# Keys, queries and attention values of a node bucket computed in the gather stage, one bucket ahead, instead of in the sort's rounds

## The chip, the cores and the metric

The kernel runs on one core of a Trainium2 chip. The metric is the device time of one launch in microseconds (us). Five engines work side by side and meet at semaphores: TensorE (PE, its weight loads shown apart as PEld), VectorE (DVE), ScalarE (ACT), GpSimd (POOL) and SyncE (SP, which here only issues DMAs).

## The reference

One relational graph layer over 6250 nodes, 200,000 edges and 16 relations, width 128. `h` is the layer norm of `x` after a relu. Every edge has a value that depends on its source node and relation alone:

```python
semb = h[src] @ tokeys.T ; oemb = h[src] @ toqueries.T ; pemb = relations[rel]
values = exp(sum(semb * pemb * oemb, axis=1) / 128)
fr = src + n * rel
values = values / segment_sum(values, fr)[fr]
output = segment_sum(values[:, None] * h[dst], fr)          # (r, n, e)
weights = einsum('rb,bij->rij', comps, bases_w)
out = x + relu(einsum('rij,rnj->ni', weights, output))
```

So per node n and relation r there is one number V[n, r] = exp(sum over e of key[n, e] * query[n, e] * relation[r, e] / 128).

## The kernel before, in words

**Tiling.** The nodes are cut into NB = 49 buckets of 128. The edges are cut into NCH = 50 chunks. Two stages follow each other.

**The sort's rounds** (`run_steps`, 52 steps, on every engine a function `step`). Step i does two things side by side. It handles bucket i: ACT normalises its nodes (`normalise`, L979), PE turns them (`transpose_h`, L1174), ACT applies the relu (`relu_ht`, L986), PE makes keys and queries (`keys_queries`, L1191 and L1192) and the messages h @ W_r for all 16 relations (`messages`, L1199, eight matmuls of 512 columns), ACT copies them out (`copy_z`, L1034) and SP stores them to the table `Z` in HBM (L301). And it sorts chunk i into streams of records by source bucket: one-hots and prefix sums on DVE (L563 to L655) and PE (L1152, L1163 to L1167, L1184), the record scatter on POOL (L453). The keys and queries go from PSUM bank 6 to SBUF by ACT (`copy_so`, L1008), are multiplied by POOL (`key_query`, L461) and multiplied by the relations on PE inside `records` (L1210, into bank 3); ACT takes the exp into `V` (L1024). Each engine runs its own list strictly in order. PE's order in a step is: transpose, sums (L1152), compact (L1184), keys and queries, prefix (L1163 to L1167), messages, records (L1210 to L1212).

**The gather stage** (after `bad < 1`; one `stepb(b)` per bucket on PE and DVE, one `bucket(b)` on ACT and SP, one `gather(b)` on POOL). SP joins the two streams of a bucket and loads its records (L322, L327). PE turns them (`turn_records`, L1267), DVE decodes them (L738) and makes the gather indices (`gather_index`, L776). POOL issues 31 to 33 indirect DMAs per bucket (L492), each of which brings 128 message rows from `Z` into one tile of `Gbuf[b % 2]`; it may start bucket b only when the sum of bucket b - 2 has been taken (`acc`). PE counts (`tables`, L1276), turns one-hots (L1286, semaphore `tp`), sums the counts (`sum_counts`, L1297 and L1298, semaphore `cs`), adds up the gathered tiles of the bucket before (`aggregate(b - 1)`, L1319, 36 tiles as 72 matmul records into bank 2, semaphore `acc` at its end) and looks the weights up (`lookups`, L1307). DVE reads the counts (`own_counts`, L784 to L790), makes the weights from V and the counts (`weights`, L799 to L815, first wait: `cs`), the one-hots of the next bucket (`tables`, L745 to L768), the output rows of the bucket before (`finish`, L833, waits for `acc`) and the weighted one-hots (`weighted_onehot`, L825). ACT copies the turned one-hots to SBUF (L1101, waits for `tp`), spreads the next bucket's relations (L1080) and copies one shared tile (L1091).

**What sets the order around the change.** All orders are written out by hand; there is no planner. PE in `stepb(b)`: turn_records(b + 1), tables(b), sum_counts(b), aggregate(b - 1), lookups(b). DVE: records(b + 1), gather_index(b + 1), own_counts(b), weights(b), tables(b + 1), finish(b - 1), weighted_onehot(b). ACT: the three copies of L1101, spread_relations(b + 1), shared_tile(b).

Of the kernel before, what the change touches and what calls it, by code (L numbers as in the profile page):

```python
# [6 lines left out]
ACT = mybir.ActivationFunctionType  # L7
# [25 lines left out]
def program(nc, x, src, dst, rel, tokeys, toqueries, relations, comps, bases_w, out):  # L33
# [40 lines left out]
    with ExitStack() as ctx:  # L74
# [3 lines left out]
        def sem(name):  # L78
# [136 lines left out]
            h th ht so_mm so_sb prod z_mm z_sb zst0 zst1 zrow v ends ends_mm nt nt_total nt_mm nt_row shared act_go join sp_go marks_sb marks_st  # L215
# [167 lines left out]
        def _(pool):  # L383
# [72 lines left out]
            def key_query(i, par):  # L456

                pool.wait_ge(s["so_sb"], i + 1)
                if dyn(i) or i >= 2:
                    pool.wait_ge(s["rec_mm"], i - 1)  # L460
                g.tensor_tensor(PR[par][:], SO[:, 0:P], SO[:, P:2 * P], ALU.mult).then_inc(s["prod"], 1)  # L461

            def step(i, par):
                if dyn(i) or 1 <= i <= NB:
                    key_query(i - 1, 1 - par)
# [57 lines left out]
        def _(dve):  # L523
# [206 lines left out]
            bad = dve.value_load(ROWI[0:1, 3 * NB:3 * NB + 1], min_val=0, max_val=16 * NB)  # L730
            with dve.If(bad < 1):
# [46 lines left out]
                def own_counts(b):  # L778
# [90 lines left out]
                gather_index(0, 0)  # L869
                tables(0, 0)  # L870
# [8 lines left out]
            with dve.If(bad > 0):  # L879

# [68 lines left out]
        def _(act):  # L949
# [54 lines left out]
            def copy_so(i):  # L1004
                act.wait_ge(s["so_mm"], i + 1)
                if dyn(i) or i >= 1:
                    act.wait_ge(s["prod"], i)
                a.copy(SO[:], bank[6][:, 0:2 * P]).then_inc(s["so_sb"], 1)  # L1008

# [7 lines left out]
            def copy_rec(i, par):  # L1017
# [5 lines left out]
                if dyn(i) or i < NB:  # L1023
                    a.activation(V[:, bass.ds(i, 1), :].rearrange("p a r -> p (a r)"), bank[3][:, 256:256 + R],  # L1024
                                 ACT.Exp, scale=1.0 / EMB).then_inc(s["v"], 1)
                else:
                    a.copy(stats[0:1, 0, 0:1], stats[0:1, 0, 1:2]).then_inc(s["v"], 1)
# [11 lines left out]
            def step(i, par, zt):  # L1039
# [10 lines left out]
                if dyn(i) or i < NB:  # L1050
                    copy_so(i)
# [21 lines left out]
            bad = act.value_load(ROWI[0:1, 3 * NB:3 * NB + 1], min_val=0, max_val=16 * NB)  # L1073
            with act.If(bad < 1):
# [19 lines left out]
                def bucket(b, par):  # L1094
# [8 lines left out]
                    if dyn(b) or b + 1 < NB:  # L1103
                        spread_relations(b + 1, 1 - par)
                        shared_tile(b, par)

                spread_relations(0, 0)
# [7 lines left out]
            with act.If(bad > 0):  # L1115
                with act.Fori(0, NCOL) as t:
# [4 lines left out]
        def _(pe):  # L1121
# [48 lines left out]
            def transpose_h(i):  # L1170
                pe.wait_ge(s["h"], i + 1)
                if dyn(i) or i >= 1:
                    pe.wait_ge(s["so_sb"], i)
# [15 lines left out]
            def keys_queries(i, par):  # L1189
                pe.wait_ge(s["ht"], i + 1)  # L1190
                t_.matmul(bank[6][:, 0:P], KQT[:, 0, :], HT[par][:], start=True, stop=True)  # L1191
                t_.matmul(bank[6][:, P:2 * P], KQT[:, 1, :], HT[par][:], start=True, stop=True)\  # L1192
                    .then_inc(s["so_mm"], 1)

            def messages(i, par):
# [6 lines left out]
            def records(i, par):  # L1202

                pe.wait_ge(s["d_sb"], i + 1)
                if dyn(i) or i >= 1:
                    pe.wait_ge(s["rec_sb"], i)
                    pe.wait_ge(s["v"], i)
# [198 lines left out]
```

## Time and profile before

| | |
|---|---|
| Time, median of 3 runs | 3077.86 us (3076.86 to 3082.03) |
| The profiled execution's own time | 3066.26 us |
| Its span | 3064.5 us |
| Mean granted TensorE clock | 0.673 |
| PE / PEld busy | 51% / 37% |
| DVE / ACT / POOL busy | 44% / 15% / 54% |
| Sort's rounds | about 50 to 390 us |
| Gather stage | about 420 to 3062 us |

The span runs from the first to the last instruction; 1.8 us of the execution lie around it. A busy share is an average over both stages. On the page PE, DVE and the DMA traffic are high in the first five of 40 slices (the rounds) and then fall to a flat pattern (the gather stage). "Issue" and "remote" in a view of waits mean that the profile shows no releaser that came last. A matmul's end is modelled, its start is recorded.

### The profile page before, as it was taken

To read this page: it belongs to the slowest core of one execution; us is meant where nothing else is said; L and a number is where in the kernel's file an instruction comes from. 1 tells how busy PE (TensorE), PEld (TensorE's weight loads), DVE (VectorE), ACT (ScalarE), POOL (GpSimd) and SP (SyncE) were. 2 spreads that over 40 slices of the span, in tenths; PEclk is the share of its full clock that TensorE was granted. 3 is DMA by queue.
4 is the path that set the end of the run, shared out by engine and by line. 5 is a ranking of instruction groups with operands and counts; after the bars stand their busy time and mean duration, and the time that the engine had idled before them with its cause. 6 is when DMAs were issued, how large, how long until landed. Compare 5 with 4: busy or idle time off the path is not lost.

```text
span 3064.5 us, 32426 instructions
## 1 busy us (share of the span) xinstructions
PE 1549.4 (51%) x9121; PEld 1129.2 (37%) x9122; DVE 1354.7 (44%) x2385; ACT 462.7 (15%) x918; POOL 1651.2 (54%) x1804
## 2 busy tenths in 40 slices
PE   4999932444344454534454443544444444544435
PEld 3666621233233333323333332333333333333324
DVE  7999934334243433424343342434334243433423
ACT  4666611000010100001010000101000010101000
POOL 3444444655646465555646565564655556464653
PEclk8999965656666665666666566666656566666667
DMA  5444411111111111111111111111111111111111
GB/s 154 156 155 155 155 55 32 46 41 42 45 36 45 36 46 39 43 42 41 45 36 45 38 44 43 40 45 37 45 38 43 44 39 45 36 46 36 45 42 29
DMA packets 99825, 170.47 MB, mean 56 GB/s; under 512 B 32491, under 2 KB 48612, under 8 KB 99575
## 3 DMA queue, kind: packets, MB, share of 16 engines
q0 software_dynamic: 51776, 104.48, 13.1%
q1 hardware_dynamic: 47672, 65.57, 6.3%
q10 hardware_dynamic: 352, 0.14, 0.0%
q8 instruction: 10, 0.16, 0.0%
q14 instruction: 15, 0.12, 0.0%
HBM read 112.24 MB, written 59.59 MB: 56 GB/s over the span
## 4 chain that ended last, share of the span: by engine, by line
another core or an unknown queue 40%; issue 21%; DVE 20%; PE 14%; SPq 2%; DMA 2%; DVEq 1%; ACT 0%; POOLq 0%; ACTq 0%
PE bank L1199 6%; DVE arena L825 4%; DVE CX L790 3%; PE bank L1184 2%; DVE stage L768 2%; DVE WC L801 2%; DVE pay_all L784 1%; PE bank L1152 1%; PE bank L1276 1%; DVE OHR L766 1%; PE bank L1319 1%; DMA RL<-bucket_streams 1%; DVE pay_all L815 1%; PE bank L1307 1%
## 5 line engine op out<-in xcount | busy, mean ns | idle before, releaser
L492 POOL DMA_INDIRECT arena<-Z_messages,IDX x1568 | 1483.0, 946 | 1137.4 <-issue 955.1
L1319 PE MATMUL bank<-arena 128*128 128x128 f32 x3528 | 695.2, 353 | 733.1 <-issue 724.9
L1319 PEld LDWEIGHTS bank<-arena 128*128 128x128 f32 x3528 | 632.5, 264 | 797.3 <-issue 795.3
L799 DVE TENSOR_SCALAR WC<-bank 128x128 f32<-128x128 f32 x49 | 14.3, 292 | 1150.5 <-remote 1149.2
L1101 ACT COPY pay_all<-bank 128x1024 bf16<-128x1024 bf16 x147 | 108.0, 807 | 2136.6 <-remote 2059.9
L1307 PE MATMUL bank<-pay_all 128*128 128x256 bf16 x882 | 179.8, 347 | 310.9 <-DVE arena L825 249.1
L825 DVE TENSOR_TENSOR arena<-stage,bank 128x512 f32<-128x512 bf16 x441 | 268.9, 681 | 12.1 <-remote 7.8
L768 DVE TENSOR_TENSOR stage<-bank,NLF 128x4608 bf16<-128x4608 f32 x49 | 242.4, 4948 | 0.0
L1307 PEld LDWEIGHTS bank<-pay_all 128*128 128x128 bf16 x882 | 86.6, 113 | 386.2 <-DVE arena L825 297.4
L1276 PE MATMUL bank<-stage,OHR 128*128 128x512 bf16 (+1 forms) x441 | 198.5, 618 | 3.2 <-DVE arena L825 3.1
L1199 PE MATMUL bank<-WT,HT 128*128 128x512 f32 x392 | 186.3, 615 | 0.0
L453 POOL DMA_INDIRECT bucket_streams<-REC,IDXW x50 | 53.7, 1074 | 200.3 <-ACT REC L1022 189.0
L1267 PE MATMUL bank<-identf,RL 36*128 36x36 f32 x49 | 14.2, 291 | 268.4 <-DMA RL<-bucket_streams 198.0
L784 DVE TENSOR_TENSOR pay_all<-bank,T 128x512 f32<-128x512 f32 x98 | 63.1, 686 | 194.8 <-issue 122.8
L1080 ACT COPY ORD<-OHR 128x2304 bf16<-128x2304 bf16 x49 | 103.5, 2112 | 258.2 <-DVE OHR L766 242.9
L1034 ACT COPY stage<-bank 128x512 f32<-128x512 f32 x196 | 114.9, 586 | 36.9 <-PE bank L1199 36.0
L1267 PEld LDWEIGHTS bank<-identf,RL 36*128 36x128 f32 x49 | 8.8, 179 | 289.8 <-issue 289.8
L738 DVE CAST RI<-bank 128x36 int32<-128x36 f32 x49 | 9.6, 196 | 229.7 <-PE bank L1267 132.6
L1297 PE MATMUL bank<-identf,VR 128*128 128x128 f32 x98 | 31.3, 414 | 146.0 <-issue 80.6
L1276 PEld LDWEIGHTS bank<-stage,OHR 128*128 128x128 bf16 (+1 forms) x441 | 56.8, 139 | 128.5 <-issue 123.2
L1199 PEld LDWEIGHTS bank<-WT,HT 128*128 128x128 f32 x392 | 64.6, 190 | 83.1 <-ACT stage L1034 59.1
L790 DVE TENSOR_REDUCE CX<-pay_all 128x128 f32<-128x1024 f32 x49 | 91.4, 1865 | 0.0
(211 smaller groups left out, 1715.5 us busy)
## 6 DMA issues: line engine op xcount, KB each, us to landing
Z_messages<-stage SPq DMA_DIRECT2D x192, 256.0 KB
arena<-Z_messages,IDX POOLq DMA_INDIRECT x1568
X<-in_x SPq DMA_DIRECT2D x4, 768.0 KB, 12.8
out<-O SPq DMA_DIRECT2D x48, 64.0 KB
bucket_streams<-bucket_streams SPq DMA_DIRECT2D x97, 18.0 KB
arena<-in_L_gnn_bases_w SPq DMA_DIRECT2D x1, 1024.0 KB, 15.0
bucket_streams<-arena SPq DMA_DIRECT2D x1, 882.0 KB
RL<-bucket_streams SPq DMA_DIRECT2D x49, 18.0 KB
```

What stands on the lines that cost most here:

```text
L492: g.indirect_dma_start(Gbuf[par][:, k, :], None, Z, bass.IndirectOffsetOnAxis(IDX[turn][:, k:k + 1], 0))\
L768: v.tensor_tensor(OHN[par], over_b(iotaP, G), over_t(NLF[:], P), ALU.is_equal)\
L784: v.tensor_tensor(own8[:, 4 * h:4 * h + 4, :], bank[h][:, :].rearrange("p (t n) -> p t n", t=4), over_t(T8[:, 4 * h:4 * h + 4], P), ALU.mu ...
L790: v.tensor_reduce(CX[:], own8.rearrange("p t n -> p n t"), AX.X, ALU.add).then_inc(s["cx"], 1)
L825: v.tensor_tensor(OW[:, n:n + 4, :], OHN[par][:, n:n + 4, :], bank[LKB[k % 2][h]][:, :].rearrange("p (t n) -> p t n", t=4), ALU.mult)\
L1034: a.copy(ZS[par][:, k * 512:(k + 1) * 512], bank[4 + k % 2][:, :]).then_inc(s["z_sb"], 1)
L1080: a.copy(ORD[:], OHR[par][:].unsqueeze(2).broadcast_to([P, G, 4, R])).then_inc(s["ord"], 1)
L1101: a.copy(ORT[:, 8 * k:8 * k + n, :].rearrange("p k e -> p (k e)"), bank[TPB[k]][:, :].bitcast(BF16)[:, 0:n * P]).then_inc(s["oht"], 1)
L1199: t_.matmul(bank[4 + k % 2][:, :], HT[par][:], WT[:, 4 * k:4 * k + 4, :].rearrange("p r i -> p (r i)"), start=True, stop=True).then_inc(s[ ...
L1276: mm = t_.matmul(bank[k % 2][0:n * R, :], OHR[par][:, k // 2 * 8:k // 2 * 8 + n, :].rearrange("p k r -> p (k r)"), OHN[par][:, 4 * k:4 * k ...
L1307: mm = t_.matmul(bank[LKB[k % 2][m // 2]][:, m % 2 * 2 * P:(m % 2 + 1) * 2 * P], ORT[:, 4 * k + m, :], BD[:].rearrange("p t n -> p (t n)") ...
L1319: return t_.matmul(bank[2][:, 0:EMB], OW[:, k, :], Gbuf[par][:, k, :], start=start, stop=stop)
```

## The change

PE, ACT and POOL lose keys, queries, product, values and their copies in the rounds. The same work is done in the gather stage for bucket b + 1 during `stepb(b)`, with one set of buffers (`H`, `HT[0]`, `SO`, `PR[0]`) and in PSUM bank 2, whose first 128 columns hold the sum of `aggregate`. The value of a bucket takes five hand-overs: DVE normalises (`nh`), PE turns (`nth`), DVE applies the relu (`nht`), PE makes keys and queries (`nkq`), DVE copies the queries and multiplies (`nq`, `npr`), PE multiplies by the relations (`nv`), ACT takes the exp (`v`). `aggregate(b - 1)` in `stepb(b)` waits for `v >= b + 2`, the exp of bucket b + 1. The second branch (`bad > 0`), which these inputs don't take, gets the same work ahead of its own.

```diff
@@ POOL: key_query and its call in step are removed
-                g.tensor_tensor(PR[par][:], SO[:, 0:P], SO[:, P:2 * P], ALU.mult).then_inc(s["prod"], 1)
@@ DVE, gather stage
+            NHT = bank[2][:, P:2 * P]
+            NKQ = bank[2][:, 2 * P:4 * P]
+            def value_normalise(b):
+                if dyn(b) or b >= 1:
+                    dve.wait_ge(s["nth"], b)
+                v.tensor_scalar(H[:], X[:, bass.ds(b, 1), :].rearrange("p a i -> p (a i)"), rstd[:, bass.ds(b, 1)],
+                                shift[:, bass.ds(b, 1)], ALU.mult, ALU.add).then_inc(s["nh"], 1)
+            def value_relu(b):
+                dve.wait_ge(s["nth"], b + 1)
+                if dyn(b) or b >= 1:
+                    dve.wait_ge(s["nkq"], b)
+                v.tensor_scalar(HT[0][:], NHT, 0.0, None, ALU.max).then_inc(s["nht"], 1)
+            def value_product(b):
+                dve.wait_ge(s["nkq"], b + 1)
+                if dyn(b) or b >= 1:
+                    dve.wait_ge(s["npr"], b)
+                v.tensor_copy(SO[:, 0:P], NKQ[:, P:2 * P]).then_inc(s["nq"], 1)
+                dve.wait_ge(s["nq"], b + 1)
+                if dyn(b) or b >= 1:
+                    dve.wait_ge(s["nv"], b)
+                v.tensor_tensor(PR[0][:], NKQ[:, 0:P], SO[:, 0:P], ALU.mult).then_inc(s["npr"], 1)
@@ DVE own_counts, before the copy into VR
+                    dve.wait_ge(s["v"], b + 1)
@@ DVE stepb
                     if dyn(b) or b + 1 < NB:
+                        value_normalise(b + 1)
                         records(b + 1)
                         gather_index(b + 1, turn)
+                        value_relu(b + 1)
                     if dyn(b) or b < NB:
                         own_counts(b)
+                    if dyn(b) or b + 1 < NB:
+                        value_product(b + 1)
+                    if dyn(b) or b < NB:
                         weights(b, par)
@@ DVE, ahead of the loop
                 records(0)
                 gather_index(0, 0)
+                value_normalise(0)
+                value_relu(0)
+                value_product(0)
                 tables(0, 0)
@@ ACT: copy_so is removed from the rounds, and from copy_rec
-                    a.activation(V[:, bass.ds(i, 1), :].rearrange("p a r -> p (a r)"), bank[3][:, 256:256 + R],
-                                 ACT.Exp, scale=1.0 / EMB).then_inc(s["v"], 1)
@@ ACT, gather stage
+            def value_exp(b):
+                act.wait_ge(s["nv"], b + 1)
+                a.activation(V[:, bass.ds(b, 1), :].rearrange("p a r -> p (a r)"), bank[2][:, P:P + R], ACT.Exp,
+                             scale=1.0 / EMB).then_inc(s["v"], 1)
@@ ACT bucket, after the three copies of L1101 (and value_exp(0) ahead of the loop)
+                        value_exp(b + 1)
                         spread_relations(b + 1, 1 - par)
                         shared_tile(b, par)
@@ PE, rounds: keys_queries removed; in records
-                    pe.wait_ge(s["prod"], i + 1)
-                    t_.matmul(bank[3][:, 256:256 + R], PR[par][:], relT[:], start=True, stop=True)
@@ PE, gather stage (NHT, NKQ as above, NV = bank[2][:, P:P + R])
+            def value_turn(b, free):
+                pe.wait_ge(s["nh"], b + 1)
+                if dyn(b) or b >= 1:
+                    pe.wait_ge(s["v"], b)
+                if free is not None:
+                    pe.wait_ge(s["o"], free)
+                t_.transpose(NHT, H[:], identf[:]).then_inc(s["nth"], 1)
+            def value_keys(b):
+                pe.wait_ge(s["nht"], b + 1)
+                t_.matmul(NKQ[:, 0:P], KQT[:, 0, :], HT[0][:], start=True, stop=True)
+                t_.matmul(NKQ[:, P:2 * P], KQT[:, 1, :], HT[0][:], start=True, stop=True).then_inc(s["nkq"], 1)
+            def value_dots(b):
+                pe.wait_ge(s["npr"], b + 1)
+                t_.matmul(NV, PR[0][:], relT[:], start=True, stop=True).then_inc(s["nv"], 1)
@@ PE aggregate(b, par), before the first matmul
+                    if dyn(b) or b + 2 < NB:
+                        pe.wait_ge(s["v"], b + 3)
@@ PE stepb
                         turn_records(b + 1, 1 - par, rl_total)
+                        value_turn(b + 1, b - 1 if dyn(b) or b >= 2 else None)
                     if dyn(b) or b < NB:
                         tables(b, par)
+                    if dyn(b) or b + 1 < NB:
+                        value_keys(b + 1)
+                    if dyn(b) or b < NB:
                         sum_counts(b)
+                    if dyn(b) or b + 1 < NB:
+                        value_dots(b + 1)
                     if dyn(b) or b >= 1:
                         aggregate(b - 1, 1 - par)
```

## Rows read from the trace of the kernel before

**Rows 1.** Engine busy time in the rounds' steady part: busy (instructions), granted clock, DMA share, GB/s

```profile
60.00:390.00 330.00, 330.00 (x2932) 227.28 (x2929) 312.58 (x427) 212.81 (x615) 142.17 (x187) 1.00 0.42 155
```

**Rows 2.** Chain of waits in the rounds: start, us, what; 45 rounds apart

```profile
64.91 0.69 PE bank L1152 x8
...
378.70 0.69 PE bank L1152 x8
```

**Rows 3.** Timeline of one round: PE, and ACT's exp

```profile
206.38 0.45 PE L1191 MATMUL bank<-HT,KQT 128*128 128x128 f32 x2
...
206.89 0.21 PE L1163 MATMUL bank<-ones,S 125*100 125x1 f16 x2
...
210.88 0.29 PE L1210 MATMUL bank<-relT,PR 128*128 128x16 f32 x2
211.02 0.22 PE L1211 MATMUL bank<-ident4k,DS 80*100 80x80 f16 x1
```

**Rows 4.** The same round on ACT

```profile
204.68 0.19 ACT L1024 ACTIVATE V<-bank 128x16 f32 x1
```

**Rows 5.** Waits from 60 to 390 us: who waited, total us, times, longest

```profile
DVE M L619 <- ACT BT L1000: 17.4, 46, 1.3
```

**Rows 6.** Waits of the whole span

```profile
ACT pay_all L1101 <- remote: 2059.9, 47, 46.1
```

**Rows 7.** Timeline of one bucket of the gather stage, 32 gathers

```profile
1493.12 0.94 POOL L492 DMA_INDIRECT arena<-Z_messages,IDX  x1 [13.90 <-issue]
...
1509.23 1.27 PE L1286 MATMUL bank<-identb,ORD 128*128 128x128 bf16 x18
...
1538.05 8.26 PE L1319 MATMUL bank<-arena 128*128 128x128 f32 x49 [0.33 <-issue]
1538.16 0.29 DVE L799 TENSOR_SCALAR WC<-bank 128x128 f32<-128x128 f32 x1 [25.38 <-remote]
1538.18 2.20 ACT L1101 COPY pay_all<-bank 128x1024 bf16<-128x1024 bf16 x3 [44.56 <-remote]
...
1547.11 0.94 POOL L492 DMA_INDIRECT arena<-Z_messages,IDX  x1 [14.29 <-issue]
```

**Rows 8.** First gather of bucket 2 and first gather of bucket 48

```profile
534.52 0.95 POOL L492 DMA_INDIRECT arena<-Z_messages,IDX  x1 [31.84 <-ACT arena L1091]
...
2995.62 0.95 POOL L492 DMA_INDIRECT arena<-Z_messages,IDX  x1 [13.53 <-issue]
```

**Rows 9.** Timeline of bucket 0, beside the gathers of buckets 0 and 1

```profile
434.89 1.18 PE L1286 MATMUL bank<-identb,ORD 128*128 128x128 bf16 x18
...
476.62 2.20 ACT L1101 COPY pay_all<-bank 128x1024 bf16<-128x1024 bf16 x3 [51.87 <-issue]
...
487.12 0.29 DVE L799 TENSOR_SCALAR WC<-bank 128x128 f32<-128x128 f32 x1 [48.79 <-remote]
```

**Rows 10.** Engine busy time in two stretches of that bucket (columns as Rows 1)

```profile
1540.00:1542.00 2.00, 2.00 (x11) 2.00 (x11) 1.77 (x7) 0.38 (x2) 0.00 (x0) 0.50 0.00 0
...
1544.00:1546.00 2.00, 2.00 (x20) 2.00 (x20) 1.73 (x3) 0.86 (x1) 0.00 (x0) 1.00 0.00 0
```

**Rows 11.** Timeline: the two sums that PE runs without a break

```profile
524.59 9.08 PE L1319 MATMUL bank<-arena 128*128 128x128 f32 x72
...
3050.19 10.92 PE L1319 MATMUL bank<-arena 128*128 128x128 f32 x72 [1.40 <-DVE arena L825]
```

**Rows 12.** Timeline of bucket 48: transposes, ACT's copies, DVE's weights

```profile
3008.45 1.18 PE L1286 MATMUL bank<-identb,ORD 128*128 128x128 bf16 x18
...
3020.64 2.20 ACT L1101 COPY pay_all<-bank 128x1024 bf16<-128x1024 bf16 x3 [24.15 <-remote]
...
3029.73 0.29 DVE L799 TENSOR_SCALAR WC<-bank 128x128 f32<-128x128 f32 x1 [17.84 <-remote]
```

**Rows 13.** Timeline: a DVE copy in SBUF and POOL's next gather

```profile
1510.78 0.23 DVE L789 COPY VR<-V 128x128 f32 x1
...
1511.87 0.95 POOL L492 DMA_INDIRECT arena<-Z_messages,IDX  x1 [0.30 <-issue]
```

More of the change, by code:

```diff
@@ L214, in program @@
             dup dense loc stat varr stdd ln ohb s8 s8_sb bt bt_sb ncount own fold half m_sum rk ohs idxw mx pos pay d_mm d_sb rec_mm rec_sb scat
-            h th ht so_mm so_sb prod z_mm z_sb zst0 zst1 zrow v ends ends_mm nt nt_total nt_mm nt_row shared act_go join sp_go marks_sb marks_st
+            h th ht nh nth nht nkq nq npr nv z_mm z_sb zst0 zst1 zrow v ends ends_mm nt nt_total nt_mm nt_row shared act_go join sp_go marks_sb marks_st
             rl0 rl1 rl_t ri dec nlf idx inv rrf ohn ohr ord vr cnt cm cx cs masks x3 w w3 bd tp oht lk ow gat0 gat1 land0 land1 land2 land3 acc o ost0 ost1
@@ L879, in _ @@
             with dve.If(bad > 0):
+                value_normalise(0)
+                value_relu(0)
+                value_product(0)
+                with dve.Fori(1, NB) as b:
+                    value_normalise(b)
+                    value_relu(b)
+                    value_product(b)
+                dve.wait_ge(s["v"], NB)
                 dve.wait_ge(s["marks_st"], 48)
@@ L1002, in copy_prefix @@
                 a.copy(COUNT[:, bass.ds(i, 1)], NCOUNT).then_inc(s["ncount"], 1)
[L1004 to L1008, printed above, removed]
             def copy_d(i, par):
@@ L1022, in copy_rec @@
                 a.activation(REC[par][:], bank[3][0:NS, 0:WIN], ACT.Copy, bias=BIG * 4097).then_inc(s["rec_sb"], 1)
-                if dyn(i) or i < NB:
-                    a.activation(V[:, bass.ds(i, 1), :].rearrange("p a r -> p (a r)"), bank[3][:, 256:256 + R],
-                                 ACT.Exp, scale=1.0 / EMB).then_inc(s["v"], 1)
-                else:
-                    a.copy(stats[0:1, 0, 0:1], stats[0:1, 0, 1:2]).then_inc(s["v"], 1)
             def copy_z(i, par, lo, hi):
@@ L1050, in step @@
                 if dyn(i) or i < NB:
-                    copy_so(i)
                     copy_z(i, par, 0, 2)
@@ L1103, in bucket @@
                     if dyn(b) or b + 1 < NB:
+                        value_exp(b + 1)
                         spread_relations(b + 1, 1 - par)
                         shared_tile(b, par)
+                value_exp(0)
                 spread_relations(0, 0)
@@ L1115, in _ @@
             with act.If(bad > 0):
+                value_exp(0)
+                with act.Fori(1, NB) as b:
+                    value_exp(b)
                 with act.Fori(0, NCOL) as t:
@@ L1172, in transpose_h @@
                 if dyn(i) or i >= 1:
-                    pe.wait_ge(s["so_sb"], i)
+                    pe.wait_ge(s["ht"], i)
                 t_.transpose(bank[6][:, 0:P], H[:], identf[:]).then_inc(s["th"], 1)
@@ L1187, in compact, with messages @@
                 mm.then_inc(s["d_mm"], 1)
-            def keys_queries(i, par):
+            def messages(i, par):
                 pe.wait_ge(s["ht"], i + 1)
[L1191 to L1195, printed above, removed]
                 for k in range(4):
@@ L1222, in step @@
                     compact(i - 1, 1 - par)
-                if dyn(i) or i < NB:
-                    keys_queries(i, par)
                 if ahead:
@@ L1254, in _ @@
             pe.wait_ge(s["rec_sb"], NCH)
-            pe.wait_ge(s["v"], NCH)
             bad = pe.value_load(ROWI[0:1, 3 * NB:3 * NB + 1], min_val=0, max_val=16 * NB)
+            NHT = bank[2][:, P:2 * P]
+            NKQ = bank[2][:, 2 * P:4 * P]
+            NV = bank[2][:, P:P + R]
+            def value_turn(b, free):
[12 more added lines that the diff above has]
+                t_.matmul(NV, PR[0][:], relT[:], start=True, stop=True).then_inc(s["nv"], 1)
             with pe.If(bad < 1):
@@ L1290, in sum_counts @@
                 def sum_counts(b):
-                    pe.wait_ge(s["v"], NCH)
+                    pe.wait_ge(s["v"], b + 1)
                     pe.wait_ge(s["cx"], b + 1)
@@ L1349, in _ @@
                 turn_records(0, 0, 16)
+                value_turn(0, None)
+                value_keys(0)
+                value_dots(0)
                 stepb(0, 0, 16)
@@ L1358, in _ @@
             with pe.If(bad > 0):
+                value_turn(0, None)
+                value_keys(0)
+                value_dots(0)
+                with pe.Fori(1, NB) as b:
+                    value_turn(b, None)
+                    value_keys(b)
+                    value_dots(b)
                 with pe.Fori(0, NCOL) as t:
```

8 lines of the change are left out of this document (removed).

## The prediction

> **What bounds the kernel now.** I read in this order. First the page's slices and the busy time by stretch, to part the two stages. Then the chain of waits and one round's timeline, for the rounds. Then the waits of the whole span, one bucket's timeline, and the same places in the first and last bucket, for the gather stage.
>
> In the rounds PE has no idle time: 330.00 of 330 us busy, at full granted clock, while DVE is busy 312.58 [rows 1]. The chain goes through PE; 45 rounds take 378.70 - 64.91 = 313.8 us, 6.97 us a round [rows 2]. DVE is close behind: its only wait is for the prefix, 17.4 us in 46 rounds, 0.38 us a round [rows 5]. So a round can shrink by 0.38 us before DVE sets it.
>
> In the gather stage a bucket takes (2995.62 - 534.52) / 46 = 53.50 us [rows 8]. Its pattern [rows 7]: POOL issues the gathers of bucket b, 32 in 39.7 us, then idles 14.29 us (so its last gather was made at 1532.8). PE's turned one-hots (18 transposes) start 16 us into the burst, but ACT, which waits for them and nothing newer, starts its copies 28 us later, at 1538.18, in the same instant as DVE, which waits for the counts (1538.16), and as the last 49 of the 72 records of PE's sum. I call this instant the release. It lies 45.04 us after the burst's start. In the burst PE's signals reach nobody from the transposes on; once the gathers are through, all arrive. ACT waited so 47 times for 2059.9 us in all [rows 6]. The mean bucket has 1568 / 49 = 32.0 gathers, so release to next burst takes 53.50 - 45.04 = 8.46 us. These 8.5 us are the rest of the sum plus POOL's start (0.8 us from 1546.31). That is the part of the path that the kernel controls.
>
> Is it PE's pile of queued sums that holds the signals up? Bucket 0 answers: no sum runs there. The transposes start at 434.89, ACT gets them at 476.62, 41.7 us later, and DVE the counts at 487.12, while gathers are issued all the time [rows 9]. With no gathers about, the sum runs through in 9.08 us at 524.59 [rows 11].
>
> **The change part by part.**
>
> *The rounds.* PE loses keys and queries, 206.89 - 206.38 = 0.51 us, and the product with the relations, 211.02 - 210.88 = 0.14 us [rows 3]: 0.65 us a round. DVE allows 0.38. POOL and ACT lose work that had slack (142 and 213 us busy of 330) [rows 1]. Gain 49 x 0.38 = 18 us; bounds 10 (another handover binds) and 49 x 0.65 = 32 (DVE gets quicker too).
>
> *Start of the gather stage.* The first value chain stands ahead of DVE's tables(0), about 3 us, beside the load of bucket 1's records, for which PE waits anyway: 0. In bucket 0 four more matmuls stand before the counts, in a stretch where four take 487.12 - 476.62 = 10.5 us [rows 9]. The lookups start 10 us later, but were held up themselves until the burst was through, so of that some 3 us stay, and 1 us of handovers in bucket 1: +4 us (0 to 10).
>
> *Each bucket, beside the gathers.* DVE's normalise and relu (0.3 us each, after the 0.29 of L799) [rows 7] and PE's transpose lie in the first 16 us of a burst, where signals still pass and DVE waits for records and counts: 0. DVE waits for `nth` ahead of its counts; behind it queue only L784 to L790, and PE's transpose comes before its tables: 0 to 0.3 us, hidden by the release. SP and POOL issue the same DMAs as before.
>
> The Trainium skill (SBUF, "Who interferes with whom") has a rule against the new normalise: a one-source DVE operation within SBUF may take the port pair it shares with GpSimd for its whole length, and descriptor generation stops. The nearest row, a copy of the same size within SBUF at 1510.78, leaves POOL's next gather at its usual 0.30 us gap [rows 13]; by the row the cost is 0, by the rule it would be at most 0.3 us x 49 = 15 us more.
>
> *Each bucket, on the path.* This is the step that decides. `aggregate(b - 1)` now waits for the exp of bucket b + 1. ACT makes that exp after its three L1101 copies, which wait for the transposes, which arrive at the release [rows 6, 7]. So none of the 72 records may start before it, where 23 did. After the release:
> - ACT: copies 2.20 us [rows 7], then the exp, 0.19 us [rows 4], and 0.1 us to PE: 2.5 us. Beside it DVE, whose wait for the keys also ends at the release, copies and multiplies (0.3 + 0.3 us) and PE makes the dots (0.29 us [rows 3], twice that on the slow clock), 1.5 us: hidden behind ACT's copies. If ACT got its copies earlier this chain would be the floor, 1.2 us.
> - PE: 72 records instead of 49. The clock is at 0.50 when they begin (11 records in 2 us) and at 1.00 from the middle on (20 in 2 us) [rows 10]. The 23 more come at full clock: 8.26 + 23 x 0.10 = 10.6 us. Unbroken sums took 9.08 and 10.92 us [rows 11]; the second began with the clock low, as here. I take 10.7; bounds 9.1 and 10.9.
> - POOL starts 0.8 us later, as now.
>
> 14.0 us in place of 8.46: +5.5 us a bucket. DVE's weights move by 0.7 us and its tables with them, but DVE's finish waits for the later `acc` anyway, so nothing else is late. It happens at each of the 46 bursts from bucket 3 to bucket 48: 46 x 5.5 = +253 us. Bounds for the step: 1.2 + 9.1 + 0.8 = 11.1 (+2.6, +120 us) and 3.2 + 10.9 + 0.9 = 15.0 (+6.5, +300 us). The last two buckets have no such wait: 0.
>
> **Sum.** Against the profiled execution's own 3066.3 us: - 18 + 4 + 253 = 3305 us. The median of the runs shown is 11.6 us above the profiled one, so 3317 us.
>
> **The rivals.**
>
> *A, the chain is in time (faster).* If in the changed kernel PE's signals pass during the burst, the exp is there some 6 us after the transposes, 22 us into it, about where the sum's first records start now, and the gather stage stays as it is. Then only the rounds count: 3078 - 18 + 1 = 3061 us. The Trainium skill points this way: SBUF, "Reading the diagram", says that PE and ACT never wait on another engine or a DMA at the ports. What for: signals do pass in the first 16 us; DVE's copy at 1510.78 comes behind the counts of the same bucket [rows 13]. Against: bucket 0, and 47 waits without exception [rows 6, 9]; that rule is about ports and no run shows it broken, but the signals come late all the same. Chance 0.10.
>
> *B, the queue was the cause after all (much faster).* If holding back the sum frees PE's signals and the sum then runs in 11 us inside the burst, POOL never waits: at least 46 x 8.46 = 390 us less, 2670 us. Bucket 0 speaks against it. 0.03.
>
> *C, signals trickle (slower, but less).* In bucket 48, with no record loads about, ACT got the transposes after 12.2 us, and the next four matmuls took 9.1 us [rows 12]. If the shifted work lets this happen in every bucket, the copies are done early, and ten more matmuls at 2.3 us still reach the release. Then 1.2 + 10.7 + 0.8 = 12.7, +4.2 us a bucket: 3255 us. 0.12.
>
> *D, more handovers cost more.* If the exp arrives only 4.5 us after the release, because each of the three hops costs some 0.7 us on engines that woke up, +7.5 us a bucket: 3409 us. 0.07.
>
> *Forecast:* 0.68.
>
> **How the numbers follow.** A change of 0.2%, 6 us, is about what a measurement of this kernel can tell from none. The forecast's own range is 3210 to 3370: its step bounds are +120 and +300, its other terms some 15 us each way, and the low end needs both favourable bounds at once. The range for 8 in 10 takes in C and goes to 3385 toward D; it leaves A and B out. Faster: A and B, 0.13, less where A's small gain is eaten up: 0.12. Same 0.01. Slower 0.87.
>
> **What would show it.** After: 6.6 us from one L1152 group to the next in the rounds, with DVE's wait for the prefix gone. In a bucket: ACT's copies still at the release, 45 us after the burst's start for 32 gathers; the exp right behind them; 72 unbroken L1319 records (no single ones in the burst), about 10.7 us; POOL's idle stretch about 19.8 us instead of 14.3. It is wrong if records of the sum start before the release (A, B), if ACT's copies come inside the burst (C), or if the exp comes over 3.5 us behind the release (D).

## The result, and the profile after

| | median | runs | profiled execution |
|---|---|---|---|
| before | 3078.48 us | 4 | 3066.3 us |
| after | 3304.1 us (3303.4 to 3305.4) | 4 | 3304.42 us, span 3302.7 |

The ratio is 1.0734 (95%: 1.0722 to 1.0746): slower, as forecast (3317, range 3185 to 3385).

Rounds. Busy time from 60 to 360 us, columns as in [rows 1]:

```profile
60.00:360.00 300.00, 300.00 (x2627) 190.80 (x2626) 299.32 (x421) 187.89 (x515) 121.60 (x137) 1.00 0.46 169
```

The chain of waits, two groups 46 rounds apart [rows 2]:

```profile
65.85 0.69 PE bank L1185 x8
...
360.25 0.69 PE bank L1185 x8
```

A round takes 294.40 / 46 = 6.40 us where it took 6.97, and DVE now has no idle time either (299.32 of 300). Its wait for the prefix [rows 5] is gone. The first gather starts at 395.70 us; it was at 421.64 before. So the rounds and what follows them up to there gave 25.9 us, not 18.

One bucket of the gather stage, the timelines of POOL, PE, DVE and ACT put together [rows 7]:

```profile
1513.15 0.95 POOL L483 DMA_INDIRECT arena<-Z_messages,IDX  x1 [18.61 <-issue]
...
1526.21 1.18 PE L1329 MATMUL bank<-identb,ORD 128*128 128x128 bf16 x18
1527.50 0.39 PE L1295 MATMUL bank<-HT,KQT 128*128 128x128 f32 x2
...
1558.61 0.29 DVE L742 COPY SO<-bank 128x128 f32<-128x128 f32 x1 [28.85 <-remote]
1558.62 2.20 ACT L1129 COPY pay_all<-bank 128x1024 bf16<-128x1024 bf16 x3 [45.86 <-remote]
1559.28 0.61 PE L1299 MATMUL bank<-relT,PR 128*128 128x16 f32 x2 [28.74 <-DVE PR L746]
1560.70 0.21 ACT L1099 ACTIVATE V<-bank 128x16 f32 x1
1561.12 11.07 PE L1365 MATMUL bank<-arena 128*128 128x128 f32 x72 [1.23 <-ACT V L1099]
...
1572.99 0.94 POOL L483 DMA_INDIRECT arena<-Z_messages,IDX  x1 [20.17 <-issue]
```

PE has made the keys at 1527.9. DVE and ACT get on 31 us later, in one instant, 45.46 us after the first of 32 gathers. The exponential follows 2.08 us behind the release, the sum 2.50 us, its 72 matmuls in one piece, 11.07 us, and the next gathers at +14.4. No single records of the sum are left in the burst (the stretch of unbroken gathers).

Bucket 2 and bucket 48 [rows 8]:

```profile
515.39 0.94 POOL L483 DMA_INDIRECT arena<-Z_messages,IDX  x1 [38.72 <-ACT arena L1119]
...
3233.18 0.94 POOL L483 DMA_INDIRECT arena<-Z_messages,IDX  x1 [16.83 <-issue]
```

(3233.18 - 515.39) / 46 = 59.08 us a bucket, where it was 53.50 (both in the profiled execution): +5.58, or +257 us. The waits of the span [rows 6]; a line is who waited, for whom, total us, times, longest:

```profile
ACT pay_all L1129 <- remote: 2102.8, 47, 47.4
DVE SO L742 <- remote: 1327.8, 46, 31.9
...
POOL arena L483 <- issue: 1161.4, 1556, 20.4
```

### The profile page after: what moved, and what is told of

It is laid out like the page before. It is cut to its first block, busy times and chain, and to the rows that moved or that the text cites. A ratio compares the mean times of both kernels' runs of the same rounds, so it can differ in the third digit from the quotient of the medians.

```text
span 3302.7 us, 32662 instructions
## 1 busy us (share of the span) xinstructions
PE 1350.1 (41%) x9121; PEld 1009.3 (31%) x9171; DVE 1398.5 (42%) x2581; ACT 449.6 (14%) x868; POOL 1627.7 (49%) x1755
## 4 chain that ended last, share of the span: by engine, by line
another core or an unknown queue 64%; PE 25%; issue 5%; DVE 2%; ACT 2%; DMA 1%; ACTq 0%; SPq 0%; DVEq 0%; POOLq 0%
PE bank L1365 16%; PE bank L1227 5%; PE bank L1217 2%; ACT pay_all L1129 1%; PE bank L1185 1%; DMA bucket_streams<-REC,IDXW 1%; DVE arena L843 0%; PE bank L1198 0%; DMA stage<-in_edge_type 0%; DVE stats L584 0%; ACT arena L1119 0%; PE bank L1207 0%; PE bank L1319 0%; DVE stage L785 0%
## 5 line engine op out<-in xcount | busy, mean ns | idle before, releaser
L742 DVE COPY SO<-bank 128x128 f32<-128x128 f32 x49 | 14.3, 291 | 1385.3 <-remote 1327.8
L1299 PE MATMUL bank<-relT,PR 128*128 128x16 f32 x98 | 29.6, 382 | 1378.0 <-DVE PR L746 1301.8
L1365 PE MATMUL bank<-arena 128*128 128x128 f32 x3528 | 512.8, 318 | 91.1 <-ACT V L1099 68.6
L1365 PEld LDWEIGHTS bank<-arena 128*128 128x128 f32 x3528 | 503.9, 233 | 96.2 <-issue 94.5
L1299 PEld LDWEIGHTS bank<-relT,PR 128*128 128x128 f32 x98 | 24.4, 308 | 1387.7 <-DVE PR L746 1311.1
L1350 PE MATMUL bank<-pay_all 128*128 128x256 bf16 x882 | 136.1, 283 | 123.7 <-DVE arena L843 109.0
L1319 PE MATMUL bank<-stage,OHR 128*128 128x512 bf16 (+1 forms) x392 | 179.3, 620 | 12.1 <-issue 10.3
L453 POOL DMA_INDIRECT bucket_streams<-REC,IDXW x50 | 70.6, 1412 | 192.8 <-ACT REC L1050 177.0
L1350 PEld LDWEIGHTS bank<-pay_all 128*128 128x128 bf16 x882 | 75.3, 99 | 172.2 <-DVE arena L843 151.4
L1217 PE MATMUL bank<-pay_all,stage 125*80 125x100 f16 x1600 | 80.7, 207 | 3.0 <-DVE stage L646 3.0
```

The lines of the kernel that those rows point to most:

```text
L1217: mm = t_.matmul(DM[:, h * NS:(h + 1) * NS], OHS[par][:, t, :], PAY[par][:, t, :, :].rearrange("p x b -> p (x b)"), start=(t % HC == 0), s ...
L1319: mm = t_.matmul(bank[k % 2][0:n * R, :], OHR[par][:, k // 2 * 8:k // 2 * 8 + n, :].rearrange("p k r -> p (k r)"), OHN[par][:, 4 * k:4 * k ...
L1350: mm = t_.matmul(bank[LKB[k % 2][m // 2]][:, m % 2 * 2 * P:(m % 2 + 1) * 2 * P], ORT[:, 4 * k + m, :], BD[:].rearrange("p t n -> p (t n)") ...
L1365: return t_.matmul(bank[2][:, 0:EMB], OW[:, k, :], Gbuf[par][:, k, :], start=start, stop=stop)
```

## The experiments

Twelve kernels in three lots of four, each lot with its own runs of the kernel before. The lots fell on three different chips. The kernel before took 3080.8 us on the first, 3077.6 on the second, and 2393.2 on the third. Times are compared within a lot only. The record doesn't name the chip of the pair above; its times are like those of the first two. Each bucket time below is of one profiled execution.

**1. The wait alone.** The kernel before, with one wait in `aggregate`; nothing is moved:

```diff
+                    if dyn(b) or b + 2 < NB:
+                        pe.wait_ge(s["oht"], b * 3 + 6)
```

> The kernel before with one line more: the sum of a bucket waits until ACT has made its three copies of the turned one-hots, the place at which the changed kernel's sum has its exp. No value work is moved. Theory W (the wait is what costs): no record of the sum before the release, 72 in one run from 2.3 us after it, release to next burst 13.5 us instead of 8.5, 46 times: about 3305 us. Theory X (the moved instructions cost, on PE, DVE and ACT beside the gathers): the wait alone changes little, under 3100 us.

Measured: 3314.9 us, ratio 1.0761 (1.0743 to 1.0779). A bucket takes 58.9 us.

```profile
1531.00 0.94 POOL L492 DMA_INDIRECT arena<-Z_messages,IDX  x1 [18.54 <-issue]
...
1576.55 2.20 ACT L1101 COPY pay_all<-bank 128x1024 bf16<-128x1024 bf16 x3 [45.94 <-remote]
1578.90 11.20 PE L1322 MATMUL bank<-arena 128*128 128x128 f32 x72 [30.84 <-ACT pay_all L1101]
...
1590.90 0.95 POOL L492 DMA_INDIRECT arena<-Z_messages,IDX  x1 [20.19 <-issue]
```

Holding the sum back until 2.35 us behind the release costs the whole loss. The moved work isn't needed for it.

**2. The moved work without the wait.** The changed kernel; turned `H`, keys and queries go to PSUM bank 4, the dots to bank 3, and PE makes the dots behind the sum. The cut below leaves out that PE now waits for the last bucket's `v` in `turn_records`, and no longer for `o` ahead of the transpose of `H`:

```diff
-            NHT = bank[2][:, P:2 * P]
-            NKQ = bank[2][:, 2 * P:4 * P]
+            NHT = bank[4][:, P:2 * P]
+            NKQ = bank[4][:, 2 * P:4 * P]
+            NV = bank[3][:, 320:320 + R]
@@ PE aggregate
-                        pe.wait_ge(s["v"], b + 3)
@@ PE stepb
-                        value_dots(b + 1)
                     if dyn(b) or b >= 1:
                         aggregate(b - 1, 1 - par)
+                    if dyn(b) or b + 1 < NB:
+                        pe.wait_ge(s["w"], b * 10 + 4)
+                        value_dots(b + 1)
@@ ACT bucket: value_exp(b + 1) behind shared_tile
```

> The changed kernel with the same moved work, but keys, queries and their input in bank 4 and the dots in bank 3, so that the sum needs no wait for the exp; the dots come after the sum on PE, the exp last in ACT's bucket. Theory W: the sum starts inside the burst again, release to next burst back at 8.5 us, and the rounds' gain stays (6.42 us a round instead of 6.97): 3078 - 26 = about 3053 us, between 3045 and 3065. Theory X: the moved instructions are all still there, so it stays near 3304 us.

Measured: 3091.1 us, ratio 1.0026 (1.0015 to 1.0038), so the loss is all but gone, yet it isn't 3053. The sum starts inside the burst again, in the median bucket 21.6 us after the first gather (21.2 in the kernel before). But a bucket takes 54.4 us. What it should be held against is kernel 3, of the same lot, below.

**3. The rounds alone.** The kernel before without keys, queries, product and exponential anywhere (the attention values are set to 1, so this part of the computation is left out).

> The kernel before without keys, queries, products and exp anywhere; V is set to 1 (the attention values are left out). It prices the rounds' part alone. Theory W: 26 us less than before, 3052 us, and the kernel with its own banks within 5 us of it. Theory X: it is 100 us or more below the one with its own banks. If the rounds' gain came from elsewhere, it is near 3078 us.

Measured: 3051.6 us, ratio 0.9906 (0.9889 to 0.9923), -29 us; the first gather at 395.16 us, a bucket 53.7 us. The rounds' gain is real and needs nothing of the new place. Kernel 2 was to lie within 5 us of this one and lies 39.5 above it. From profile to profile, a bucket takes 0.69 us more there (54.43 and 53.74), 32 us in 46 buckets, and the way from the first gather to bucket 2's 5.4 us more. So the moved work does cost time in kernel 2, more than the rounds give back.

**4. The exponential ahead of ACT's copies** in the changed kernel:

```diff
                 def bucket(b, par):
+                    if dyn(b) or b + 1 < NB:
+                        value_exp(b + 1)
                     act.wait_ge(s["tp"], b + 1)
@@ behind the three copies
-                        value_exp(b + 1)
```

> The changed kernel with one edit: ACT makes the exp before its three copies instead of behind them. The exp is then bound by the handovers behind the release (product 0.6, dots 0.6 us). Theory W with ACT's order as the term: the sum starts 1.5 us after the release instead of 2.5, 1.0 us less in 46 buckets, 3304 - 46 = about 3258 us. If the chain of handovers is what delays the sum (rival D of the prediction), nothing changes: 3304 us.

Measured: 3275.4 us, ratio 1.0634 (1.0616 to 1.0651), by the ratios 31 us less than the changed kernel. The sum starts 1.81 us behind the release (mean of 43 buckets) and not 2.51, and a bucket takes 58.41 us and not 59.08: of 0.70 us that the sum starts earlier, 0.67 are won. I had expected 1.0 us; DVE's copy and product and PE's dots, which ACT's copies had covered, are the path now.

**5. Three matmuls in place of the 18 transposes**, in the kernel before (the turned one-hots are left out):

```diff
-                    for k in range(G // 2):
-                        mm = t_.transpose(bank[TPB[k // 8]] ..., ORD[:, 2 * k:2 * k + 2, :, :] ..., identb[:])
+                    for k in range(3):
+                        mm = t_.matmul(bank[TPB[k]][:, :], identb[:], OHN[par][:, 4 * k:4 * k + 4, :] ..., start=True, stop=True)
```

> The kernel before, with 3 matmuls of 512 columns in place of the 18 transposes of the one-hots; the turned one-hots are left out, so the weights that are looked up are not the reference's. In the kernel before, ACT and DVE get the signals of the transposes and of the counts 45 us after a bucket's first gather, though the records of the matmuls stand at about 16 us. Theory T (the gathers hold back whatever TensorE reports late in a burst): nothing changes, VectorE's first operation on the counts starts 45.0 us after the first gather of 32, a bucket still takes 53.5 us, the whole 3080 us (3060 to 3090). Rival M (the 18 small transposes themselves take the time and their records are placed too early): the signal comes by 20 us after the first gather, the sum starts in the burst and ends before it does, a bucket takes 45 us, the whole 2690 us.

Measured: 3001.1 us, ratio 0.9751 (0.9734 to 0.9767). Neither theory holds. One bucket, its first gather at 1464.31 us; PE, ACT and DVE put together:

```profile
1476.73 1.46 PE L1286 MATMUL bank<-stage,identb 128*128 128x512 bf16 x3
1480.26 2.20 ACT L1101 COPY pay_all<-bank 128x1024 bf16<-128x1024 bf16 x3 [16.31 <-remote]
...
1480.92 0.39 PE L1298 MATMUL bank<-CX,RS 128*128 128x128 f32 x2
1481.72 5.10 PE L1319 MATMUL bank<-arena 128*128 128x128 f32 x29 [0.41 <-issue]
1487.22 0.27 PE L1319 MATMUL bank<-arena 128*128 128x128 f32 x1 [0.40 <-issue]
1490.02 0.27 PE L1319 MATMUL bank<-arena 128*128 128x128 f32 x1 [2.53 <-issue]
...
1491.44 0.29 DVE L799 TENSOR_SCALAR WC<-bank 128x128 f32<-128x128 f32 x1 [11.16 <-remote]
...
1506.86 0.37 PE L1319 MATMUL bank<-arena 128*128 128x128 f32 x1 [1.74 <-issue]
1508.96 0.37 PE L1319 MATMUL bank<-arena 128*128 128x128 f32 x1 [1.73 <-issue]
1509.67 5.52 PE L1319 MATMUL bank<-arena 128*128 128x128 f32 x34 [0.34 <-issue]
```

ACT gets the signal of the 3 matmuls 2.1 us behind their end (mean of 45 buckets 3.5), DVE that of the next four 10.1 us behind theirs (mean 10.8), well inside the burst. Then the sum: 29 records at once, 9 single ones 2.7 us apart (1487.22 to 1508.96), the rest at the release. 3 + 4 + 29 = 36 matmuls ran ahead before the single ones began. So the signals aren't shut off during the gathers. They come as if in order, at about one matmul per 2.7 us. With 18 transposes ahead that would be 49 us (an estimate), which is over the burst, and there everything comes at once. Bucket 0 of the kernel before fits: 41.7 us for 18, 10.5 for the next four [rows 9], 2.3 and 2.6 each.

**6. A pause.** The kernel before; GpSimd waits for the transposes' signal after a bucket's 14th gather (the expectation says 15th; the numbering starts at 1):

```diff
                     for k in range(FIRSTK, FLOOR):
                         tile(k)
+                        if k == 14:
+                            pool.wait_ge(s["tp"], b + 1)
+                            pool.sem_inc(s["pool_go"], 1)
```

> The kernel before, with GpSimd waiting after its 15th gather of a bucket for the signal of the bucket's last transpose, and issuing the rest after it. Theory T (TensorE's signals get through when the gathers already issued have drained, 1.41 us each): the signal arrives 21 to 23 us after the first gather, where it arrives at 45 us in the kernel before; the burst gets 2 to 5 us longer, a bucket takes 54 to 59 us, the whole 3110 to 3330 us. Rival M (the time is the matmuls' own, and the gathers have nothing to do with it): the signal still arrives at 45 us, the other 17 gathers come after it, a bucket takes some 75 us, the whole 4000 us or more.

Measured: 2800.3 us, ratio 0.9095 (0.9080 to 0.9110): 9% faster, better than either theory had it. One bucket, POOL, PE, DVE and ACT put together:

```profile
1418.74 0.94 POOL L492 DMA_INDIRECT arena<-Z_messages,IDX  x1 [4.17 <-issue]
...
1431.22 1.18 PE L1289 MATMUL bank<-identb,ORD 128*128 128x128 bf16 x18
1436.20 10.69 PE L1322 MATMUL bank<-arena 128*128 128x128 f32 x72
1439.13 0.29 DVE L802 TENSOR_SCALAR WC<-bank 128x128 f32<-128x128 f32 x1 [4.37 <-remote]
1439.15 2.20 ACT L1104 COPY pay_all<-bank 128x1024 bf16<-128x1024 bf16 x3 [20.79 <-remote]
1439.84 0.94 POOL L492 DMA_INDIRECT arena<-Z_messages,IDX  x1 [3.93 <-remote]
...
1467.11 0.29 DVE L836 SCALAR_TENSOR_TENSOR O<-bank,X 128x128 f32<-128x128 f32 x1 [15.88 <-remote]
...
1467.70 0.94 POOL L492 DMA_INDIRECT arena<-Z_messages,IDX  x1 [4.43 <-ACT arena L1094]
```

The signals come 20.4 us after the first gather. In 40 of the 47 buckets from bucket 2 on it is 20.05 to 20.44 us for 14 gathers, where the kernel before has 45.0 us for 32; in the other seven it is 23 to 31 us. The sum runs through in 10.69 us, mostly beside the second stretch, but its end is reported only 27.3 us after that stretch of 19 began, again when its gathers are through. A bucket takes 47.2 us in a stretch of 16 (712.3 to 1467.7) and 48.3 us in the mean of 46. What is saved is 5 to 6 of the 8.5 us between release and next gathers: the sum, 72 matmuls in one piece, now starts 2.9 us ahead of the release and runs beside gathers. How long TensorE's signals are held thus goes by the unbroken run of gathers before them.

**7. The sum ahead of the counts**, in the kernel before (in PE's `stepb`, `aggregate(b - 1)` moves ahead of `tables(b)` and `sum_counts(b)`).

> The kernel before, with TensorE's weighted sum of the last bucket put ahead of this bucket's counts and transposes. The order, not the amount of work, changes. Theory T (the sum starts 20 us into the burst, its end is reported only when the burst has drained, as are the counts): the next gathers start about 1 us after that, and a bucket's 8.5 us between the release and the next gather go; but the counts come behind the sum, so weights, lookups and weighted one-hots (about 14 us on VectorE) stand ahead of the next sum. A bucket takes 46 to 50 us, the whole 2740 to 2920 us. Rival C (the chain counts, weights, lookups, one-hots, sum, acknowledged back to GpSimd is in series and lengthens): the bucket takes 60 us or more, the whole 3380 us.

Measured: 3298.0 us, ratio 1.0719 (1.0701 to 1.0737). The theory's order never came about. One bucket, POOL's first gather at 1462.29 us; PE and DVE:

```profile
1463.44 1.18 PE L1286 MATMUL bank<-identb,ORD 128*128 128x128 bf16 x18
1467.69 0.39 PE L1298 MATMUL bank<-CX,RS 128*128 128x128 f32 x2
1468.11 0.29 DVE L799 TENSOR_SCALAR WC<-bank 128x128 f32<-128x128 f32 x1 [1.10 <-PE bank L1298]
...
1508.05 0.29 PE L1267 MATMUL bank<-identf,RL 36*128 36x36 f32 x1 [23.58 <-DMA RL<-bucket_streams]
1509.16 10.20 PE L1319 MATMUL bank<-arena 128*128 128x128 f32 x72 [0.83 <-issue]
```

The counts, now first in the burst, reach DVE at once, 5.8 us into it. But PE's next bucket begins with the records, which it gets only 45.8 us after the first gather, and the sum stands behind them. A bucket takes 58.4 us. The load isn't slow: SP issues it at 1506.89, 1.2 us before PE's record. It is issued late. SP's steps before it, from the store of the output rows to the first join and from there to the load, take 17.5 and 10.3 us in the mean of 46 buckets, and 3.4 and 6.1 in the kernel before, where the load is issued 12 us into a burst and not 45. So signals pass freely in a burst's first microseconds, and deep in a burst SP's chain is slow too. What holds SP there I can't tell from the trace.

**8. VectorE's product behind the weights**, in kernel 2 (in DVE's `stepb`, `value_product(b + 1)` moves behind `weights(b, par)`; PE's wait for `w` goes).

> The changed kernel with its keys, queries and dots in a bank of their own (so without the wait for the exponential ahead of the sum), and with VectorE's product of keys and queries behind the bucket's weights and not ahead of them. Theory: with the product ahead, a bucket took 54.4 us, 0.9 more than before, of which 0.6 is the product; with it behind, 53.6 to 53.9 us, the whole 3056 to 3068 us, faster than both kernels by 0.4 to 0.8%, since the rounds keep their 26 us. Rival: the sum sets the gap, not VectorE, and the product's place is nothing: 54.4 us and 3091 us.

Measured: 3087.6 us, ratio 1.0036 (1.0023 to 1.0048), like kernel 2. The rival holds. Parted by when the transposes start, in the 22 buckets where it is under 18 us into the burst, a bucket less 1.41 us for each gather takes 8.69 us; kernel 2 has 8.95 (26 buckets), the kernel before 8.13 (33). In the others it is 9.72, 9.78 and 8.99; and those are 23, 19 and 12 of 45. Kernel 3, which has none of the moved work, has 8.37 (30 buckets) and 9.01 (16 buckets). Held against it, the product's place is worth 0.3 us, another 0.3 stay unexplained, and the rest is that more buckets get their records late. Why they do I didn't settle.

**9 to 12, on the third chip.** The changed kernel with the pause of 6 (e10); kernel 2 with it (e11); the kernel before with a memset of 32x1 on GpSimd ahead of each of 30 gathers (e12); kernel 2 with the pause behind the 20th gather and for the sum's signal (`acc`, e13).

> The changed kernel, with GpSimd waiting after a bucket's 14th gather for the signal of the bucket's last transpose, as in the kernel before with a pause (2800 us, 47.3 us a bucket). Theory: the change cost time because its exponential waited for signals of TensorE that came only when the gathers had drained; with the pause the signal of the keys comes at about 20 us, the exponential at 23 us, and the sum runs from there on beside the second half of the gathers. If it ends before that half has drained, a bucket takes 47.3 us here too and the rounds' 26 us are won: 2775 us. Rival S: the sum, started 3 us into the second stretch of gathers and not 3 us before it, runs out of its first instructions, trickles and ends after the drain, 3 to 6 us more in each of 46 buckets: 2910 to 3050 us. I hold S the likelier for this one.

> The changed kernel with its keys, queries and dots in a bank of their own, the exponential not ahead of the sum, and the same pause for the transposes' signal. Theory: the sum starts at 18 us as in the kernel before with the pause, a bucket takes 47.3 to 47.8 us, and the rounds' 26 us less 7 at the start are left: 2780 to 2805 us. Rival S, that any work added to TensorE's list in a bucket pushes the lookups or the sum behind the drain: 48.5 us a bucket or more, 2835 us or more.

> The kernel before, with one memset of 32x1 on GpSimd ahead of each of a bucket's first 30 gathers, to make its step between gathers 1.45 us and not 1.25. Theory B (TensorE is held up by the gathers that are issued and not yet drained, 1.41 us each): no backlog builds up, all its signals are prompt, the sum ends about 32 us into the bucket and the next gathers start as soon as the last are issued: 46 to 48 us a bucket, the whole 2730 to 2830 us. Rival: it is held up while gathers run at all, however slowly they are issued: the signals come at the end of the burst as before, 30 x 0.2 us less what drains beside, 53.5 to 58 us a bucket, the whole 3077 to 3280 us.

> The changed kernel with its own bank, as above, and the pause after a bucket's 20th gather, for the signal of the last bucket's sum. All signals of TensorE's work in the bucket come in that pause, the sum's too, so the next bucket's gathers need not wait. Theory: the sum's 72 matmuls trickle in the first stretch and end after its 20 gathers have drained, at 28 us, plus the sum's rest, up to 8 us: 45.5 us of draining and 8 to 10 us of pause, 53 to 55 us a bucket, 3080 us, if the sum trickles as it does in the kernel before; 46.5 us a bucket and 2750 us if it doesn't.

| | us | ratio (95%) |
|---|---|---|
| before | 2393.2 | |
| e10 | 2366.4 | 0.9888 (0.9871 to 0.9904) |
| e11 | 2366.5 | 0.9885 (0.9869 to 0.9902) |
| e12 | 2393.0 | 1.0000 (0.9990 to 1.0009) |
| e13 | 2365.7 | 0.9884 (0.9867 to 0.9900) |

All four expectations were for the behaviour of the first two chips, and none came true. Of e10, the waits (as above), POOL's first gather and its last:

```profile
POOL arena L483 <- issue: 477.5, 1567, 0.3
PE bank L1368 <- ACT V L1102: 586.9, 47, 14.6
```

```profile
394.76 0.99 POOL L483 DMA_INDIRECT arena<-Z_messages,IDX  x1 [9.32 <-DVE IDX L796]
...
2351.76 0.94 POOL L483 DMA_INDIRECT arena<-Z_messages,IDX  x1 [0.30 <-issue]
```

and of one of its buckets, PE and DVE:

```profile
1424.97 0.39 PE L1344 MATMUL bank<-CX,RS 128*128 128x128 f32 x2
1425.40 0.29 DVE L820 TENSOR_SCALAR WC<-bank 128x128 f32<-128x128 f32 x1 [0.30 <-PE bank L1344]
```

Here POOL issues 1568 gathers without one gap over 0.3 us: 1957 us at 1.249 each, 40.0 us a bucket. Deep in the stream DVE gets PE's counts in 0.3 us. The pause never held POOL, so e10 is in effect the changed kernel, which itself wasn't run on this chip. The sum does wait for the exponential, 586.9 us in all, and it costs nothing: all of it lies beside POOL. What is left is the first gather at 394.8 and not 422.0 (e12's): 27 us, and that is the whole difference to the kernel before. In e12 the memset (0.11 us) went into the 0.31 us that POOL leaves between gathers, so the step stayed 1.25 us and the run says nothing about pacing.

The fastest kernels are thus, for chips like the first two, number 6 (0.9095, run on the second alone), and for the third e10, e11 and e13, which I can't tell apart. The changed kernel with the pause was never run on a chip of the first kind. By the pieces it should beat number 6 by up to the rounds' 26 us; that is argued, not shown.

## Why the prediction was right, and where its reasons weren't

- *Rounds, -18 foretold, -26 measured.* The term was mis-sized. It took DVE's wait alone, 0.38 us a round, and a round lost 0.57: DVE gets quicker too, which stood in the bounds only. DVE's one-hots (OHB) took 1085 ns in the mean of 50, and in the changed kernel 977. In the kernel before, the 46 that overlap POOL's product take 1094 ns and the four that don't 980. One of the 46, and that product of keys and queries, which is gone after:

```profile
206.36 1.09 DVE L563 TENSOR_TENSOR OHB<-iotaB,q 125x1600 f16<-125x1600 f16 x1
...
206.86 0.90 POOL L461 TENSOR_TENSOR PR<-SO 128x128 f32<-128x128 f32 x1
```

  0.38 + 0.11 of the 0.57 us a round are so accounted for; the rest are small gaps. The Trainium skill (SBUF, "Who interferes with whom") says that a DVE instruction with two inputs in SBUF contends with a GpSimd instruction that reads SBUF; the trace agrees, 1094 ns with the overlap and 980 without.
- *Start of the gather stage, +4 (0 to 10).* From the first gather to bucket 2's it took 119.7 us and not 112.9: +6.8. Kernel 3, without the moved work, took 113.8.
- *Release to exponential.* Foretold 2.5 us from release to sum; measured 2.51 (43 buckets). Kernels 1 and 4 show it as the path from both sides.
- *The sum in one piece.* Foretold 10.7 us; mean of 40 records 10.38 (8.28 to 11.22). With POOL's 0.8, release to next gather is 13.7 us, not 14.0.
- *The release itself.* Held at 45.04 us for 32 gathers; measured 45.39. Most of this 0.35 us isn't the change's: kernel 3, with nothing moved, has 45.28. The profiled execution of the kernel before was itself 11.6 us faster than the median, 0.25 us for each of 46 buckets, and I read the baseline from it. So 5.58 a bucket against 5.5 is 0.3 us too much for the sum and a baseline that was too low. With the medians, 3304.1 - 3078.5 = 225.6 us, less the other two terms (-25.9 and +6.8), a bucket lost about 5.3 us.
- *The whole.* Between the profiled executions, -25.9 + 6.8 + 257 = 238 us, where 239 was foretold: the rounds came out 8 us lower, the other two 7 us higher. That they cancel is luck. The 12.9 us that 3317 lies too high are mainly the 11.6 us that I added for the median: they didn't come back, since the changed kernel's profiled execution lies at its median.
- *Everything beside the gathers at 0*: right for the size in the changed kernel, as kernels 1 (58.9 us a bucket with nothing moved) and after (59.1) stand 0.2 us apart. It isn't right in general: without the wait nearly the same work costs 0.7 us a bucket (kernels 2 and 3). The normalise left GpSimd's gap between gathers at 0.30 us, so the up to 15 us that the prediction set beside its sum by a rule of the Trainium skill (SBUF, "Who interferes with whom") didn't appear.
- *"In the burst PE's signals reach nobody from the transposes on."* Right in its effect, wrong as a mechanism. The signals come in order, as far as kernel 5 and bucket 0 show, one matmul per 2.3 to 2.7 us; 18 transposes are too many to get through. Rival C had this mechanism and I gave it 0.12, since I reckoned that shorter shifts in load would let it happen. It took fewer matmuls.
- *What it all hung on*: that the chip behaves as in the one trace. On the third chip rival A is true, the exponential is in time, and the change is in effect 1.1% faster (e10); A gave 3061 from the same 18 us. Its "some 6 us after the transposes" isn't true there, though. In the bucket shown of e10 the exponential comes 17 us after them, at 1437.63, since ACT's own list has a copy ahead of it that waits for gathers. No harm comes of it, as POOL is the path.

## What to carry to other kernels

Ahead of moving a chain of hand-overs beside a long stream of indirect gathers, look in the trace for when each engine's signals arrive, not when its work ends; what waits for a held signal moves to the end of the stream with all that is queued behind it. If signals are held, break the stream in two with a wait on one that matters: here that won 9% on the one chip where it was tried, more than any placing of the work. And run the pair on more than one chip before you keep a change whose worth is a wait, since the same two kernels differed by +7.3% on one and, in effect, -1.1% on another.

## What the hardware showed that I hadn't expected

- Two kinds of chip. In the pair's own profile of the kernel before, the release follows the gathers at 43.6, 45.0 and 46.4 us for 31, 32 and 33 of them, 1.41 us each, though POOL issues one per 1.25 us. Two of the three lots behave like it. The third has none of it, and the same kernel takes 2393 us and not 3078. Each lot ran on one chip, so whatever else differed between the lots can't be parted from the chip.
- It isn't the data. In the bucket of [rows 7] the gathers' bytes had all moved by 1535, 3 us before the release at 1538.16 (columns as in [rows 1]):

```profile
1523.00:1533.00 10.00, 1.49 (x4) 1.15 (x4) 0.00 (x0) 0.00 (x0) 7.56 (x8) 0.50 0.20 52
1533.00:1535.00 2.00, 0.37 (x1) 0.29 (x1) 0.00 (x0) 0.00 (x0) 0.00 (x0) 0.50 0.13 33
1535.00:1537.00 2.00, 0.72 (x2) 0.57 (x2) 0.00 (x0) 0.00 (x0) 0.00 (x0) 0.50 0.00 0
```

  52 GB/s is what one gather of 64 KB per 1.25 us makes, and e12 on the third chip moves the same. So "drained" in my expectations is the wrong word. Nor do the gathers' completions lag, as far as the trace has them: in each of 46 buckets of the kernel before, the last one on record comes 2.2 to 2.6 us after the last gather is issued, nearly 4 us before the release. That completions and PE's signals share a path there, and that the first go ahead, would fit all of it. It is a guess; no run shows it.
- A rival that I left untested is the recording itself. A gather's completion counts in 16 steps. Of the 25,088 steps the trace of the kernel before has 4922, a fifth; that of e12 on the third chip has 24,560, or 98%. So on the chips that hold PE's signals, most records of the gathers' signals are missing too. Every timed run of the twelve kernels has a recorded span and clock, so none is known to have run unrecorded, and whether the signals are also late then stays open.
- PE's records run some 33 to 36 matmuls ahead of its signals (36 in kernel 5), then slow to one per 2 to 3 us. A matmul's record in such a stretch tells when it was let in, not when others hear of it. The Trainium skill (Perfetto Trace Analysis, "Per-engine timelines") says that the reported span leaves out how a semaphore update travels; here what lies between the end of the transposes' record and ACT's start is 40.6 us in bucket 0 [rows 9].
